# Attention heads in groups of three and two: maxima through the query tile, half the weighted sums, and a normalisation moved from DVE to ACT

## What is computed

```python
x = x + tanh(g_xattn[0]) * xattn0(layernorm(x), ctx)      # rotary positions, softmax over the 77 keys
x = x + tanh(g_ffn[0])   * ffn0(layernorm(x))             # 8 experts, the best one per token
x = x + tanh(g_xattn[1]) * xattn1(layernorm(x), ctx, mask) # biases, masked softmax
x = x + tanh(g_ffn[1])   * ffn1(layernorm(x))             # 8 experts, the best two, SiLU gate

def attention(q, k, v):                                    # per head
    w = softmax(q @ k.T / sqrt(8))                         # layer 1: masked keys out
    return concat(w @ v) @ Wo + bo
```

## Time and profile before

| | us |
|---|---|
| median of 3 runs | 451.59 |
| the runs | 450.32 to 460.82 |
| span of the profiled execution | 464.2 |

### The profile page before, as it was taken

The page is one execution under the profiler, slowest core; times in us unless marked ns, Lnnn a source line. Parts: engine busy times, 40 slices in busy tenths (PEclk is TensorE's granted clock), DMA queues, the critical chain, the costliest instruction groups (busy, mean ns, idle before and its releaser), DMA issues.

```text
span 464.2 us, 7008 instructions
## 1 busy us (share of the span) xinstructions
PE 314.7 (68%) x1932; PEld 228.1 (49%) x1932; DVE 264.1 (57%) x916; ACT 136.3 (29%) x302; POOL 152.2 (33%) x172
## 2 busy tenths in 40 slices
PE   2468999989754095751467999999530298888920
PEld 2236555545353094640256566654320297777820
DVE  2768668773675244353367667765545066665634
ACT  2412354535313033220103454354200033333300
POOL 3211212051423134561102102165766134555550
PEclk9767799999985579795567999999855599999985
DMA  7434032100000867823231313000103677988708
GB/s 268 126 74 118 12 80 52 43 11 19 17 8 29 224 215 215 243 73 90 62 85 36 71 27 85 14 24 23 42 29 100 213 244 236 299 249 289 235 12 269
DMA packets 39997, 52.93 MB, mean 114 GB/s; under 512 B 7177, under 2 KB 24334, under 8 KB 39968
## 3 DMA queue, kind: packets, MB, share of 16 engines
q1 hardware_dynamic: 33648, 45.03, 33.7%
q0 software_dynamic: 3584, 6.36, 3.9%
q10 hardware_dynamic: 2736, 1.20, 0.9%
HBM read 35.58 MB, written 9.64 MB: 97 GB/s over the span
## 4 chain that ended last, share of the span: by engine, by line
PE 21%; DVE 8%; issue 7%; DMA 6%; SPq 4%; POOL 4%; ACT 1%; POOLq 0%; DVEq 0%; ACTq 0%
POOL routed L445 3%; PE ps_s L750 2%; PE ps_a L730 2%; DMA xt<-routed 2%; PE ps_a L731 2%; PE ps_s L821 2%; SPq L342 2%; PE ps_s L751 2%; PE ps_t L705 2%; PE ps_n L765 2%; PE ps_a L838 1%; PE ps_d L765 1%; PE ps_t L821 1%; DMA probs<-expert_out 1%; DMA routed<-pay,slot 1%
## 5 line engine op out<-in xcount | busy, mean ns | idle before, releaser
L463 POOL DMA_INDIRECT expert_out<-yo,rows_at x64 | 63.0, 984 | 81.5 <-DVE yo L1179 63.6
L529 ACT ACTIVATE probs<-ps_s 103x512 f32<-103x512 f32 (+1 forms) x96 | 56.3, 597 | 56.8 <-PE ps_s L751 53.3
L445 POOL DMA_INDIRECT routed<-pay,slot x48 | 48.4, 1009 | 58.3 <-DVE slot L1132 47.8
L1025 DVE TENSOR_REDUCE negm<-ps_a 128x4 f32<-128x308 f32 x128 | 55.1, 470 | 19.5 <-PE ps_a L731 18.0
L750 PE MATMUL ps_s<-qs,ks 128*103 128x512 f32 (+1 forms) x96 | 46.2, 481 | 2.0 <-ACT augT L522 1.2
L731 PE MATMUL ps_a<-ks,qs 128*128 128x308 f32 x128 | 43.1, 374 | 5.9 <-DVE negm L1025 5.6
L421 POOL TENSOR_SCALAR ve<-mv 128x4 f32<-128x4 f32 x16 | 4.0, 251 | 116.0 <-DVE mv L975 116.0
L751 PE MATMUL ps_s<-augT,aug 128*103 128x512 f32 (+1 forms) x96 | 39.6, 412 | 0.0
L838 PE MATMUL ps_a<-cst,xt 128*128 128x128 f32 x32 | 11.1, 355 | 39.8 <-DMA xt<-routed 38.2
L731 PEld LDWEIGHTS ps_a<-ks,qs 128*128 128x128 f32 x128 | 28.9, 227 | 15.4 <-DVE negm L1025 6.6
L821 PE MATMUL ps_s<-xT,probs 128*128 128x128 f32 x208 | 32.5, 299 | 2.9 <-DVE xT L1190 1.7
...
## 6 DMA issues: line engine op xcount, KB each, us to landing
...
qs<-qhl SPq DMA_DIRECT2D x128, 64.0 KB, 2.0
...
```

The costliest lines, as they stand in the source:

```text
L445: pool.indirect_dma_start(out=routed[l], out_offset=bass.IndirectOffsetOnAxis(ap=slot[c][:, t:t + 1], axis=0), in_=pay[c][:, t, :], in_off ...
L463: pool.indirect_dma_start(out=expert_out[l], out_offset=bass.IndirectOffsetOnAxis(ap=rows_at[i % SHORT][:, :], axis=0), in_=yo[i % SHORT][ ...
L529: nc.scalar.activation(probs[n % 2][0:KSIZE[j], s, :], ps_s[(NS * n + s) % SCORE_BANKS][0:KSIZE[j], :], ACT.Exp, scale=SCALE).then_inc(exp ...
L1025: nc.vector.tensor_reduce(negm[:, i, g * HPG:(g + 1) * HPG], a[:, 0:GK].rearrange("p (h k) -> p h k", h=HPG), AX.X, ALU.max, negate=True). ...
```

## The change

Heads are grouped anew: four groups of three heads (231 columns and a zero one) and two groups of two (154), six in all. 96 rows of `qs` hold a group's queries (high twice, low twice, interleaved), rows 96 to 101 the split maxima of its heads, and the same rows of `ks` ones per head, so that one product of 102 rows gives score minus maximum.

- `spread_q` issues twelve DMAs, whose source names each row twice. A new `spread_max` issues six more a batch, from `augT` into `qs`; `scores` waits for them. `mark_heads` writes the ones once.
- `scores`: one matmul in layer 0; in layer 1 a first one adds mask by `aug`. Tiles have 116, 115 and 77 keys.
- `scores_for_max`: a unit covers two groups in one bank (two matmuls of 256 columns; in layer 1 a mask product of 512 columns before them); 12 units a batch, maxima over 462 or 308 elements; they fall due in seven steps instead of ten, `split` and `augment` two steps earlier.
- `weigh`: four matmuls a round; the denominators come as further columns of the values (`value_constants` on POOL sets these once).
- `divide` takes the place of `recip_den`, `widen_rd` and `weigh_out`: numerators and denominators are both turned to tokens, divided there by DVE, turned back, copied by ACT (`copy_att`).
- `normalise2` moves from DVE to ACT (four activations, scale and shift per token); the shift comes from two small instructions on POOL.
- The masked keys are written straight from PSUM by `take_keys`; `mask_keys` is gone. `probs` is one ring of 16 slots instead of two buffers of 12.

```diff
-GROUPS, HPG = 4, 4
+GROUPS, TRIPLES = 6, 4
+HPG = [3, 3, 3, 3, 2, 2]
+AUG = 256
+UNITS = GROUPS // 2 * TPB
-    "split": -3, "augment": -2, ...
+    "split": -5, "augment": -4, ...
-MAX_UNITS = [1, 2, 2, 2, 1, 2, 2, 2, 1, 1]
+MAX_UNITS = [2, 2, 2, 2, 2, 1, 1]
...
             def spread_q(n):
...
-                        for c in range(2):
-                            rows = 64 * c + 32 * half
-                            sp.dma_start(qs[n % 3][rows:rows + 32, g, :].bitcast(F32), qhl[half][32 * g:32 * g + 32, :].bitcast(F32)).then_inc(qspread[n % 3][g], 16)
+                        sp.dma_start(qs[n % 3][48 * half:48 * half + 2 * count, g, :].bitcast(F32),
+                                     bcast(qhl[half][q0:q0 + count, :].bitcast(F32), 1, 2)).then_inc(qspread[n % 3][g], 16)
+            def spread_max(n):
+                sp.wait_ge(augT_ok, n + 1)
+                for g in range(GROUPS):
+                    sp.dma_start(qs[n % 3][STACK:ROWS, g, :].bitcast(F32),
+                                 augT[n % 2][MAXIMA * g:MAXIMA * (g + 1), :].bitcast(F32)).then_inc(qspread[n % 3][g], 16)
...
                 for b in range(NB):
                     spread_q(NB * l + b)
+                    if l == 0 and b == 0:
+                        mark_heads()
+                    if b:
+                        spread_max(NB * l + b - 1)
                     if l == 0 and b == 1:
                         sp.dma_start(w[1][:, :], w_in[1]).then_inc(ld_w[1], 16)
+                spread_max(NB * l + NB - 1)
                 load_tiles(l)
...
+            def shift_back(n):
+                link(nc.gpsimd.tensor_tensor(shift2[:, :], mv2[:, :, 0], rstd2[:, :], ALU.mult))
+                nc.gpsimd.tensor_scalar(shift2[:, :], shift2[:, :], -1.0, None, ALU.mult).then_inc(rstd2_ok, 1)
...
+            def copy_att(n):
+                act.wait_ge(att_tr, n + 1)
+                nc.scalar.activation(att[:, :], ps_t[:, :], ACT.Copy).then_inc(att_ok, 1)
+            def normalise2(n):
+                act.wait_ge(rstd2_ok, n + 1)
+                b = n % NB
+                for i in range(TPB):
+                    last = nc.scalar.activation(pay[0][:, b * TPB + i, 0:D], x[:, b * TPB + i, :], ACT.Identity,
+                                                bias=shift2[:, i:i + 1], scale=rstd2[:, i:i + 1])
+                last.then_inc(nrm2_ok, 1)
...
             def take_keys(l):
-                    nc.scalar.activation(ksp[:, g * NB * KEYS:(g + 1) * NB * KEYS], ps_s[0][:, 0:NB * KEYS], ACT.Copy).then_inc(k_even, 1)
+                    for h in range(HPG[g]):
+                        last = nc.scalar.activation(ks_heads(g, h), ps_s[0][0:STACK, 0:NB * KEYS].rearrange("p (b k) -> p b k", b=NB),
+                                                    ACT.Copy, scale=hm[0:STACK, h:h + 1])
+                    last.then_inc(k_even, 1)
...
             def scores_for_max(n, u):
...
-                    nc.tensor.matmul(bank[:, 0:GK], maskT[:, i * P:(i + 1) * P], aug[:, g, :], start=True, stop=False)
-                nc.tensor.matmul(bank[:, 0:GK], qs[n % 3][:, g, i * P:(i + 1) * P], ks[:, g, b, :], start=not l, stop=True).then_inc(ring_full, 1)
+                    nc.tensor.matmul(bank[:, :].rearrange("p (c k) -> p c k", c=2), maskT[0:KEYS, i * P:(i + 1) * P], bcast(aug[0:KEYS, :], 1, 2), start=True, stop=False)
+                for c in range(2):
+                    g = 2 * v + c
+                    if i == 0:
+                        pe.wait_ge(qspread[n % 3][g], 48 * (n // 3) + 32)
+                    last = nc.tensor.matmul(bank[:, c * AUG:(c + 1) * AUG], qs[n % 3][0:STACK, g, i * P:(i + 1) * P],
+                                            ks_group(g, b)[0:STACK, :], start=not l, stop=not l or c == 1)
+                last.then_inc(ring_full, 1)
...
             def scores(n, s):
...
-                if s == 0:
-                    pe.wait_ge(augT_ok, n + 1)
+                if lo == 0:
+                    pe.wait_ge(qspread[n % 3][g], 48 * (n // 3 + 1))
...
-                nc.tensor.matmul(bank, ks[:, g, b, lo:hi], qs[n % 3][:, g, :], start=True, stop=False)
-                nc.tensor.matmul(bank, aug[:, g, lo:hi], augT[n % 2][:, :], start=False, stop=True).then_inc(sc_full, 1)
+                if l:
+                    nc.tensor.matmul(bank, aug[0:KEYS, lo:hi], maskT[0:KEYS, :], start=True, stop=False)
+                nc.tensor.matmul(bank, ks_group(g, b)[:, lo:hi], qs[n % 3][0:ROWS, g, :], start=not l, stop=True).then_inc(sc_full, 1)
...
             def weigh(n, j):
...
-                for bank, lhs in ((ps_n, lambda g: vb[0:kk, j, b, 32 * g:32 * g + 32]), (ps_d, lambda g: hmv[0:kk, j, :])):
-                    for g in range(GROUPS):
-                        last = nc.tensor.matmul(bank[32 * g:32 * g + 32, :], lhs(g), probs[n % 2][0:kk, j * GROUPS + g, :],
-                                                start=j == 0, stop=j == KT - 1)
+                bank = ps_n if j < 2 else ps_d
+                for i in range(QUADS):
+                    last = nc.tensor.matmul(bank[32 * i:32 * i + 32, :], vb[0:kk, j, b, 32 * i:32 * i + 32], prob(n, j * QUADS + i)[0:kk, :],
+                                            start=j != 1, stop=j != 0)
...
+            def divide(n):
+                a = ring()
+                dve.wait_ge(num_tr, n + 1)
...
+                nc.vector.tensor_scalar(rd[:, :, 3], singles[:, :, HD], 1e-30, None, ALU.max)
+                link(nc.vector.tensor_scalar(rd[:, :, 0:3], triples[:, :, 24:27], 1e-30, None, ALU.max))
+                link(nc.vector.reciprocal(rd[:, :, :], rd[:, :, :]))
+                nc.vector.tensor_tensor(dst[:, :, 24:32], singles[:, :, 0:HD], bcast(rd[:, :, 3], 2, HD), ALU.mult).then_inc(ring_used, 1)
+                nc.vector.tensor_tensor(dst[:, :, 0:24].rearrange("p q (h d) -> p q h d", d=HD), triples[:, :, 0:24].rearrange("p q (h d) -> p q h d", d=HD),
+                                        bcast(rd[:, :, 0:3], 3, HD), ALU.mult).then_inc(s_dve, 1)
```

More of the change, by code:

```diff
@@ L31 @@
 HEADS, HD = 16, 8
-GROUPS, HPG = 4, 4
-GK = HPG * KEYS
-KT = 3
-KROWS = 103
-KSIZE = [min(KROWS, GK - KROWS * j) for j in range(KT)]
-NS = KT * GROUPS
+SLOT_HEADS, QUADS = 4, 4
+GROUPS, TRIPLES = 6, 4
+HPG = [3, 3, 3, 3, 2, 2]
+FIRST_HEAD = [0, 3, 6, 9, 12, 14]
+HEAD_ORDER = [4 * i + a for i in range(QUADS) for a in range(3)] + [4 * i + 3 for i in range(QUADS)]
+TK = 3 * KEYS + 1
+GK = [TK, TK, TK, TK, 2 * KEYS, 2 * KEYS]
+KS_AT = [NB * sum(GK[:g]) for g in range(GROUPS + 1)]
+STACK = 96
+MAXIMA = 6
+ROWS = STACK + MAXIMA
+KT = 3
+KROWS = 116
+KSIZE = [KROWS, 3 * KEYS - KROWS, KEYS]
+NS = KT * QUADS
+PROBS = 16
+AUG = 256
+UNITS = GROUPS // 2 * TPB
+KS_END = KS_AT[GROUPS] - GK[GROUPS - 1] + AUG
 SCALE = float(HD) ** -0.5
@@ L96 @@
 VALUES_AT = [[-2, -1, 0], [LAST + 17, LAST + 20, LAST + 21]]
-BLOCKS_AT = [-17, LAST + 27]
 SET_UP_AT = -14
@@ L188, in two_layers @@
         dens = sb("dens", [P, SEQ])
-        rd = sb("rd", [P, TPB, HEADS])
-        rdx = dens
+        rd = sb("rd", [P, TPB * QUADS, SLOT_HEADS])
+        att_tok = dens
         att = sb("att", [P, SEQ])
+        maskf = nums[:, 0:TPB * KEYS].rearrange("p (t k) -> p t k", t=TPB)
         st2 = sb("st2", [P, TPB, 6])
@@ L479, in _ @@
                     for b in due("stats2", k):
-                        power(var2, ve2, rstd2, rstd2_ok, n0 + b)
+                        power(var2, ve2, rstd2, s_pool, n0 + b)
+                        pool.wait_ge(s_pool, chain.next() + 1)
+                        shift_back(n0 + b)
                     for b in due("normalise2", k):
@@ L521, in copy_augT @@
                     act.wait_ge(sc_full, NS * (n - 1))
[L522 removed]
+                used = GROUPS * MAXIMA
+                nc.scalar.activation(augT[n % 2][0:used, :], ps_t[0:used, :], ACT.Copy).then_inc(augT_ok, 1)
             def exps(n, s):
[L525 removed]
+                j = s // QUADS
                 act.wait_ge(sc_full, NS * n + s + 1)
[L527 to L529 removed]
+                behind = KT * n + j + 1 - PROBS // QUADS
+                if s % QUADS == 0 and behind >= 1:
+                    act.wait_ge(pv_ok, behind)
+                nc.scalar.activation(prob(n, s)[0:KSIZE[j], :], ps_s[(NS * n + s) % SCORE_BANKS][0:KSIZE[j], :], ACT.Exp, scale=SCALE).then_inc(exp_ok, 1)
             def copy_nd(n):
@@ L639, in _ @@
                         copy_nd(n0 + b)
-                    for b in due("widen", k):
-                        widen_rd(n0 + b)
+                    for b in due("rden", k):
+                        copy_att(n0 + b)
+                    for b in due("normalise2", k):
+                        normalise2(n0 + b)
                     for b in due("turn2", k):
@@ L878, in _ @@
                         pe.wait_ge(s_masked, 1)
-                        transposes(lambda i: augt[1][:, i, :], mask_tr, maskT_ok, 1)
+                        if reader:
+                            pe.wait_ge(*reader[-1])
+                        reader.append((maskT_ok, 1))
```

(8 more changed lines are left out.)

292 lines of the change are left out of this document (153 added, 139 removed).

## The result

The kernel after takes 515.08 us (median of 4 runs, 510.82 to 518.73), the kernel before 451.66 us beside it: a ratio of 1.140, 95% interval 1.129 to 1.151. Slower, and far outside the predicted 442 to 467.

The account below looks back on a forecast made before the run. TensorE (PE) was taken to set the pace mid-attention, with latency chains in each layer's last stretch. Layer 0 at -1.2 and layer 1 at +3.6 gave +2.4 on a 464.2 us span, scaled to 454.0 us; range 442 to 467.

Parts of the forecast that it names:

- The hand-over: H(n+1), next batch's first query step on ACT, to S(n), batch n's first score matmul: at least 10.3 us.
- eleven issues: SP's further query DMAs ahead of the maxima within a hand-over, 0.63 us each, 7.0 us.
- over 12: Sign of being wrong: hand-overs, H(n+1) to S(n), under 8 us or over 12.
- 1.75 us per wait: PE's clock loss after each wait for maxima: 3.5 us at half rate, charged where PE is the bound, layer 1.
- Rival (b): PE stays at 1.2 GHz longer after each wait; +11, 465 us; chance 0.30.
- Middle clock under 0.8: Sign of being wrong: the clock row of attention's middle stretches under 0.8.
- The normalisation on ACT: Four 128x128 activations per batch on ACT, 1.3 us taken, hidden except in the tails.
- S(3) to the last sum: Layer 0, batch 3's first score matmul to the last weighted sum: -5.4 us, bounds -7.5 and -2.
- S(2) to S(3): Layer 0, first score matmul of batch 2 to that of batch 3: -3.2 us, bounds -6.7 and 0.
- S(0) to H(2): Layer 0, batch 0's first score matmul to the start of batch 2's queries on ACT: -2.3 us.
- The tails: Each layer's end, after its last weighted sum: +3.8 us in layer 0, +1.9 in layer 1.
- The scale: Whole kernel: median of runs 451.59 us is 0.973 of the profiled span, turning 466.6 into 454.0 us.

Follow-up runs that it names:

- e5: Kernel after with 26 extra float32 matmuls placed where PE sits idle; 490.32 us.
- e13: Kernel after with maxima between the queries on SP, second normalisation on DVE, layer 1's keys behind the plan, padding rows ahead of them; 482.29 us.
- e8: Kernel after with rows of zeros added: mask products of 128 rows for 77, score products 128 for 102; 512.33 us.
- e12: e7 with second normalisation on DVE, layer 1's keys behind the plan (padding rows first), and all score and maxima products over 128 rows; 457.92 us.
- e10: Kernel before with layer 0's second score product taking 32 rows instead of 128; 464.26 us, ratio 1.022.
- e2: Kernel after with maxima copied by ACT into augT instead of sent by DMA, and a second product per score tile; 523.03 us.
- e7: e2 with layer 0's second score product taking 113 rows instead of 36, the added rows zero; 487.21 us.
- e9: Kernel before, unchanged, run again for a second profile; 453.36 us, span 451.5.
- e6: Kernel after with the spreading of layer 1's keys moved from before layer 0's last router to behind its plan; 511.21 us.
- e1: Kernel after with SP issuing the maxima of a batch between two halves of the next batch's queries; 498.17 us.
- e3: Kernel after with the second normalisation back on DVE and no shift on GpSimd; 507.15 us.
- e14: e13 with 17 extra matmuls added where PE idles; 471.49 us.

## Why the prediction was wrong

**The hand-over: mechanism right, term mis-sized.** The place and the queue order are as foretold, and PE waits ahead of S(1), S(2), S(5) and S(6). But the hand-overs are 12.15, 12.41, 11.94 and 11.95 us, not 10.3. The wrong term is eleven issues "x 0.63": in the first hand-over they took 8.3 us, not 7.0. SP's timeline, six of the eight issues of 48 rows (24 rows, each named twice), then the four of 32 rows (16, each named twice):

```profile
60.30 4.85 SPq L370 DMA_DIRECT2D qs<-qhl  x6
...
65.20 2.54 SPq L370 DMA_DIRECT2D qs<-qhl  x4
```

Those of 48 rows follow each other at 0.81 us, those of 32 at 0.65, close to the 0.63 of plain ones in the earlier trace rows: the longer form costs more, the doubling by itself does not. Besides, `low_q` took 1.08 us for the 0.69 taken. Landing (67.78 to 69.84, 2.06) was as taken from the row. The prediction's own sign of being wrong, "over 12", was met by two of the four.

**The clock: the step that failed.** I charged 1.75 us per wait, and that only where PE is the bound, 3.5 us in all. It came from one idle spell of 1.99 us, after which the earlier trace rows show 2.8 us at half rate. After S(1) it was 9.8 us (69.84 to 79.67). In the four stretches behind the hand-overs the length times the clock that was missing comes to 4.9, 6.2, 7.2 and 7.4 us, 26 in all, an estimate from their windows; e5 got 3.7, 6.5 and 5.5 of it back behind S(1), S(5) and S(6). Rival (b) had the mechanism, but with too small a price (3 to 5 us a stretch in layer 1 and 2 in layer 0, where against the forecast the four lost 5 to 9) and for the hand-overs alone. "Middle clock under 0.8" was met too (0.61 to 0.75).

Why the 2.8 us did not carry over is shown in part. A longer idle spell is not needed for it: in e13 17.4 us at 1.2 GHz followed 1.58 us of idle. The change also altered what PE does behind the wait: products of 96, 102 and 77 rows for 128, and half the weighted sums. Wider products brought clock back in layer 1 of e8 and in three stretches of e12. But layer 0 of e8 did not move, 32-row products in e10 kept the clock, and layer 1 ran at two clocks in e2 and e7 with the same products. So the rows are the likely cause, and it stays open what else decides. The saved work, 4.7 us of PE a batch in layer 0, was counted at the full clock; the products that are left take longer at the lower one.

**The normalisation on ACT: the second failed step.** I hid it behind ACT's busy share (9.40 of 20.68). Its cost is not in its length, four in 1.64 us, against 1.3 taken. It is in its place in ACT's queue: 8 us in the kernel after, 15 alone. The estimate of 1.6 from the Trainium skill (ScalarE: Activation LUTs, What ACT_TABLE_LOAD costs) is borne out by the trace, by these 1.64.

**S(3) to the last sum (-5.4, was +1.5), S(2) to S(3) (-3.2, was +3.3)** failed with these two: PE idles 2.91 us up to 141.20 for the normalisation on ACT, and the clocks are 0.68 and 0.74.

**S(0) to H(2)** came as forecast (-2.2 for -2.3) by luck: the 15.09 us it was taken from were long in that one execution, and against e9 it grew by 0.3.

**The tails** grew as said, 5.2 and 1.3 for 3.8 and 1.9; the keys in front of the router, taken at 3.0, are 4.6 by e6. To S(0) it was +4.5 for +2.4, whose cause was not looked for. DVE's units at 0.58 us on the mean are as taken (6.7 over 12 is 0.56).

**The scale** of 0.973 carried the long stretches of the first profile, 12 us of its span, into the forecast. With e9's span the same sum of +2.4 gives 456 us for 454, so this is not where the 61 us went.

Accounting, from 515: the order on SP is worth 17 us (e1), the normalisation 8 (e3), the keys some 5 (from e6's tail, which alone gained nothing), and the three together measured 482 (e13). With the remaining idle spells filled it is 471 (e14). On another way, with full rows and no maxima by DMA, it is 458 (e12). How much of that last figure is clock is not shown, since its products, waits and issues differ from those of e13. In the kernel after itself the products can't all be widened (rows 96 to 101 hold the maxima of another batch when the units run), so that was not tried.
